# Attention and ternary FFN on one core: another order of work in the fronts of both batches

## The reference

```
q, gate = split(x @ Wq)          # 8 heads of 64, and a gate of the same width
k, v    = x @ Wk, x @ Wv         # 2 key/value heads of 64, each for 4 query heads
q, k    = rotary(q), rotary(k)   # on 16 of the 64 features of a head
o       = softmax(q k^T / 8) v   # full attention over 2048 keys
x       = layernorm(x + (o * silu(gate)) @ Wo)
h       = bitlinear(x, w_fc) + 0.05 * x @ v_lr^T @ fast_b^T @ u^T     # hidden 1024
x       = layernorm(x + bitlinear(relu(h)^2, w_proj))
```

## Time and profile before

| | us |
|---|---|
| median of 3 runs | 1777.85 (1777.14 to 1778.02) |
| the profiled execution | 1775.12 |
| its span, first to last instruction | 1773.3 |
| TensorE busy | 1670.2 (94%) |
| VectorE busy | 1390.5 (78%) |
| GpSimd busy | 989.9 (56%) |
| ScalarE busy | 742.0 (42%) |
| first score matmul of batch 0 / of batch 1 | 91.52 / 957.60 |
| mean granted TensorE clock | 0.972 of full |

### The profile page before, as it was taken

How to read it: one execution, slowest core, us unless ns; L and a number is a source line. 1 busy time by engine, 2 the same in 40 slices (tenths; PEclk the granted TensorE clock), 3 DMA queues, 4 the chain that set the end, 5 groups by cost and what they waited for, 6 DMA issues and landing times.

```text
span 1773.3 us, 26408 instructions
## 1 busy us (share of the span) xinstructions
PE 1670.2 (94%) x6902; PEld 817.4 (46%) x6902; DVE 1390.5 (78%) x1692; ACT 742.0 (42%) x1407; POOL 989.9 (56%) x765
## 2 busy tenths in 40 slices
PE   5699999999999999999868999999999999999996
PEld 3444444444444444447744444444444444444585
DVE  6668888888888888757766788888888888885587
ACT  1244444444444444444422444444444444445352
POOL 0546666666666665653334566666666666657342
PEclk8799999999999999999987999999999999999998
DMA  4600101000000000020043010000000000000001
GB/s 163 159 18 23 23 23 24 22 22 22 23 22 22 22 20 19 1 78 24 25 115 84 18 29 23 23 23 22 22 22 23 22 22 22 19 1 1 25 25 48
DMA packets 36916, 59.76 MB, mean 34 GB/s; under 512 B 6624, under 2 KB 17264, under 8 KB 36288
## 3 DMA queue, kind: packets, MB, share of 16 engines
q1 hardware_dynamic: 36800, 58.50, 12.6%
HBM read 20.07 MB, written 4.19 MB: 14 GB/s over the span
## 4 chain that ended last, share of the span: by engine, by line
PE 75%; DVE 10%; issue 8%; ACT 2%; DMA 2%; POOL 1%; SPq 1%; DVEq 0%; ACTq 0%; POOLq 0%
PE ob L578 24%; PE trio L566 16%; PE trio L567 11%; PE sc L533 8%; PE trio L513 6%; PE trio L672 3%; DVE acc L328 2%; PE trio L589 2%; DVE maxp L1059 2%; PE sc L639 2%; ACT probs L824 2%; DMA acc<-in_x 1%; PE ob L687 1%; PE trio L687 1%; PE trio L525 1%
## 5 line engine op out<-in xcount | busy, mean ns | idle before, releaser
L328 POOL TENSOR_TENSOR acc<-acc,probs 128x512 f32<-128x512 f32 x448 | 577.2, 1288 | 435.1 <-DVE acc L328 377.2
L824 ACT ACTIVATE probs<-trio 128x512 f32<-128x512 f32 x1024 | 530.0, 603 | 654.5 <-PE trio L567 556.4
L1059 DVE TENSOR_REDUCE maxp<-sc 128x2 f32<-128x1024 f32 x472 | 575.1, 1218 | 138.6 <-PE sc L535 137.1
L578 PE MATMUL ob<-probs,v_sb 128*64 128x512 f32 x2048 | 495.8, 605 | 0.0
L328 DVE TENSOR_TENSOR acc<-acc,probs 128x512 f32<-128x512 f32 x448 | 429.9, 960 | 81.3 <-ACT probs L824 76.7
L566 PE MATMUL trio<-qa,kab 128*128 128x512 f32 x1024 | 459.8, 449 | 3.6 <-DMA qb<-mrow 3.6
L567 PE MATMUL trio<-qb,kab 128*128 128x512 f32 x1024 | 405.0, 396 | 0.0
L566 PEld LDWEIGHTS trio<-qa,kab 128*128 128x128 f32 x1024 | 192.4, 188 | 322.6 <-issue 210.7
L578 PEld LDWEIGHTS ob<-probs,v_sb 128*64 128x64 f32 x2048 | 123.9, 136 | 241.6 <-issue 178.8
L533 PE MATMUL sc<-kab,qa 64*128 64x512 f32 x512 | 197.1, 460 | 29.1 <-DVE maxp L1198 16.0
L567 PEld LDWEIGHTS trio<-qb,kab 128*128 128x128 f32 x1024 | 194.1, 190 | 23.4
(11 more groups left out here) (122 smaller groups left out, 1420.4 us busy)
## 6 DMA issues: line engine op xcount, KB each, us to landing
qa<-high_sb SPq DMA_DIRECT2D x128, 128.0 KB, 2.3
qb<-low_sb SPq DMA_DIRECT2D x64, 128.0 KB, 2.3
tables_sb<-in_tables SPq DMA_DIRECT2D x34, 128.0 KB, 2.4
xT_sb<-in_xT SPq DMA_DIRECT2D x2, 2048.0 KB, 10.2
acc<-in_x SPq DMA_DIRECT2D x8, 512.0 KB, 4.2
out_y<-acc SPq DMA_DIRECT2D x8, 512.0 KB, 3.1
kab<-acc SPq DMA_DIRECT2D x24, 128.0 KB, 2.4
rot_sb<-raw_sb SPq DMA_DIRECT2D x72, 32.0 KB, 1.8
```

What stands on the lines that cost most here:

```text
L328: ops.tensor_tensor(total, total, part, ALU.add).then_inc(summed, 1)
L578: mm = nc.tensor.matmul(ob[hd * D:(hd + 1) * D, :], v_sb[:, t, kv * D:(kv + 1) * D], probs[:, t % RING, hd * CHUNK:(hd + 1) * CHUNK], star ...
L824: nc.scalar.activation(probs[:, t % RING, hd * CHUNK:(hd + 1) * CHUNK], score_bank(t, hd), ACT.Exp, scale=float(D) ** -0.5).then_inc(probs ...
L1059: nc.vector.tensor_reduce(two_columns(p, j), MAX_PAIRS[j % 2], AX_X, ALU.max).then_inc(maxed, 1)
```

## The change

The two fronts get another order, and some of their work another engine; the arithmetic stays.

- **Loads by first use.** SP loads k weights, the first 512 columns of x, w_fc, the q weights of pair 0, then x in chunks; w_proj, v weights, the rest of wq and wo follow between the first swaps. Five small loads go onto ScalarE's queue. Semaphores are split so that each user waits for its own load.
- **Set-up inside the front.** The low-rank product, the transposes and their copies stand between the stages and the maxima of front 0; in between go the first projections.
- **Front order** k0, q0, k1, k2, k3, q1, q2, and all rotary work on GpSimd, with the low part of a stage behind the rotary work of later ones.
- **High parts first.** A stage's two high parts that the maxima need (`k_early`, `q_early`) are placed by ScalarE right behind the rounding; they have their own semaphore, and the maxima wait for it alone. The other four placements stay on SP (`place_rest`), and the scores of a unit wait for them.
- **Stage q2** is rounded, split and placed in the first unit of attention.
- **Unrolled**: both batches, and all 128 cycles of attention of each.
- **Next batch in the FFN.** The first two projections of batch 1 stand on TensorE between the up and the down matmuls of the last chunk of batch 0; their copies follow on ScalarE behind the last squares, their swaps on SP ahead of the store of that chunk's output.

```diff
-    for i in range(HEAD):
-        emit(0, i // CYCLES, i % CYCLES)
-    with eng.Fori(0, NCH - 1) as c:
-        for i in range(HEAD, HEAD + PAIRS * CYCLES):
-            emit(c, i // CYCLES, i % CYCLES)
-    for i in range(HEAD, PAIRS * CYCLES):
-        emit(NCH - 1, i // CYCLES, i % CYCLES)
+    for unit in range(UNITS):
+        for y in range(CYCLES):
+            emit(unit // PAIRS, unit % PAIRS, y)
...
+        FRONT = [("k", 0, 0), ("q", 0, 1), ("k", 1, 2), ("k", 2, 3), ("k", 3, 0), ("q", 1, 1), ("q", 2, 0)]
...
+        def place_early(eng, stage, b, targets):
+            slot = stage[0]
+            eng.wait_ge(rounded[slot], done(uses(stage, b) + 1))
+            for part, hd, dst in targets:
+                eng.dma_start(raw_words(dst), raw_words(part[slot][hd * D:(hd + 1) * D])).then_inc(early[slot], 16)
...  (SP)
+            sp.dma_start(wk_sb[:, :, :], ...).then_inc(k_loaded, 16)
+            load_x(0, 0)
             sp.dma_start(wfc_nat, w_fc.rearrange("(j p) c -> p j c", p=P)).then_inc(wfc_loaded, 16)
+            sp.dma_start(wqg_sb[:, :, 0:P], wq_v[:, :, 0:P]).then_inc(q_loaded, 16)
+            load_x(0, 1)
+            sp.wait_ge(tables_cleared, 2)
...
+                front_tables(4, b)
+                front_swap(4, b)
+                front_rest(0, b)
+                front_tables(5, b)
+                front_rest(1, b)
+                front_swap(5, b)
+                front_rest(2, b)
+                front_rest(3, b)
+                front_rest(4, b)
+                front_tables(6, b)
+                front_swap(6, b)
+                sp.wait_ge(ones_set, 3)
                 place_max(b, 0, 0)
+                front_rest(5, b)
...  (TensorE)
+            for b in range(BATCH):
+                if b == 0:
+                    front_project(0, b)
+                    front_project(1, b)
+                    setup_gated_rank()
+                front_project(2, b)
+                front_project(3, b)
+                if b == 0:
+                    setup_low_rank()
+                    setup_wfc_transposes()
+                front_project(4, b)
+                front_project(5, b)
...
                 front_maxima(0)
+                if b == 0:
+                    setup_wp_transposes(0)
+                else:
+                    v_half(2, b)
                 front_maxima(2)
...
+                max_transpose(b, 0, 0, ob[:, :])
                 for i in range(2, LEAD):
                     front_pair(1, i)
+                if b == 0:
+                    v_half(5, b)
+                    v_half(6, b)
+                    v_half(7, b)
+                    front_project(6, b)
...
+                    if c == NCH - 1 and b < BATCH - 1:
+                        front_project(0, b + 1)
+                        front_project(1, b + 1)
                     ffn_down(first_n + c, range(JT - 2))
...  (ScalarE, batch 0)
+                    front_round(0, b)
+                    setup_wfc_copies()
+                    front_round(1, b)
+                    front_round(2, b)
+                    front_copy(4, b)
+                    setup_wp_copies(0)
+                    front_round(3, b)
+                    setup_wp_copies(1)
+                    setup_scale_copy()
+                    front_copy(5, b)
+                    front_round(4, b)
+                    copy_v(0, b)
+                    copy_v(1, b)
+                    front_round(5, b)
+                    copy_v(2, b)
+                    front_copy(6, b)
+                    copy_v(3, b)
...  (GpSimd)
+                front_rope(0, b)
+                front_rope(1, b)
+                front_rope(2, b)
+                front_low(0, b)
+                front_rope(3, b)
+                front_low(1, b)
+                front_rope(4, b)
+                front_low(2, b)
+                front_low(3, b)
+                front_rope(5, b)
+                front_low(4, b)
+                front_low(5, b)
+                front_rope(6, b)
```

More of the change, by code:

```diff
@@ L510, in project, with setup_scale_row @@
+            def setup_scale_row():
+                pe.wait_ge(q_copied, done(5))
+                for i in range(2):
+                    mm = nc.tensor.matmul(trio[i * D:(i + 1) * D, 0, 0:HID], ones[:, :], wp_scale[:, :],
+                                          start=True, stop=True)
+                mm.then_inc(setup_pe, 1)
             def project(w, col, chunk, semaphore, bank):
@@ L741, in _ @@
+                for slot in range(SLOTS):
+                    stage = front([0, 1, 2, 3][slot]) if slot else front(4)
+                    pe.wait_ge(placed[slot], placed_before(stage, b, 1))
+                pe.wait_ge(ones_set, 3)
+                pe.wait_ge(q_copied, done(b * STAGES + PRO))
                 pe.wait_ge(v_copied, done((b + 1) * TILES))
@@ L748, in _ @@
                 first_n = b * NCH
+                pe.wait_ge(wo_loaded, 16)
                 output_projection(first_n, 0)
@@ L781, in _ @@
[L781 to L786 removed]
+            act.dma_start(fbT_sb, fast_bT).then_inc(small_loaded, 16)
+            for dst, src in ((v_lr_sb, v_lr), (gate_sb[:, :], gate), (uT_sb, uT), (ident[:, :], ident_in)):
+                act.dma_start(dst, src).then_inc(small_loaded, 16)
@@ new lines, in setup_gate, with setup_wfc_copies @@
+            def setup_gate():
+                act.wait_ge(small_loaded, 16 * 5)
+                act.wait_ge(setup_pe, 1)
+                nc.scalar.activation(bv_sb, sc[0:RANK, 3, 0:HID], ACT.Copy, scale=gate_sb[0:RANK, 0:1])\
+                  .then_inc(setup_act, 1)
+            def setup_wfc_copies():
+                act.wait_ge(setup_pe, 3)
+                for h in range(HC):
+                    for q in range(2):
+                        last = nc.scalar.copy(wfcT[:, h, q * CHUNK:(q + 1) * CHUNK], sc[:, 2 * h + q, :])
+                last.then_inc(setup_act, 1)
@@ new lines, in setup_wp_copies, with setup_scale_copy, copy_stage @@
+            def setup_wp_copies(half):
+                act.wait_ge(setup_pe, 4 + half)
+                for q in range(2):
+                    j = 4 * half + 2 * q
+                    last = nc.scalar.copy(wpT[:, j:j + 2, :], V_BANKS[q].rearrange("p (a c) -> p a c", a=2))
+                last.then_inc(setup_act, 1)
+            def setup_scale_copy():
+                act.wait_ge(setup_pe, 6)
+                nc.scalar.copy(wp_scale[:, :], trio[:, 0, 0:HID]).then_inc(setup_act, 1)
+            def copy_stage(stage, number, b, bank):
@@ L833, in emit @@
                     exponential(b, c, p, 2 * y + 1)
+                    if y == 0 and first(c, p):
+                        round_stage(front(6), b)
                     if y == 0 and behind_exists(c, p):
@@ new lines, in front_round @@
+            def front_round(s, b):
+                what, n = FRONT[s][0:2]
+                if b >= 1 and s == 1:
+                    act.wait_ge(ffn2_ready, done(2 * b * NCH))
+                if b >= 1 and s == 2:
+                    act.wait_ge(res_done, done(b * NCH * TILES))
+                if s == 3:
+                    act.wait_ge(y_stored, 16 * (NCH * b + 1))
+                round_stage(front(s), b)
+                place_early(act, front(s), b, k_early(n) if what == "k" else q_early(n))
@@ L946, in emit @@
                     add_exponentials(pool, nc.gpsimd, b, c, p, 2 * y + 1, 0, sum_a, sum_b)
+                    if y == 1 and first(c, p):
+                        rope_low(nc.gpsimd, front(6), b)
                     if y == 1 and behind_exists(c, p):
```

438 lines of the change are left out of this document (246 added, 192 removed).

## The result

The kernel after takes **1691.38 us** (median of 4 runs, 1690.12 to 1692.52), the kernel before 1777.49 us (1777.04 to 1778.02) beside it; the ratio is 0.9515 with a 95% interval of 0.9499 to 0.9532. The forecast was 1736 us (1717 to 1757): the change gained 86 us, twice the 42 forecast.

The account below looks back on a forecast made before the run. Attention was taken as bound by TensorE's own stream, the fronts by chains across engines. Front 0 -20, front 1 -22 and attention 0 gave -42 from 1775.12: 1733, plus 2.7 for the median: 1736 us (1717 to 1757).

Parts of the forecast that it names:

- Unrolled attention: Attention's 256 cycles: neither the jump back nor fresh code costs a visible amount; 0, bounds 2 us either way.
- Front 0: Start of batch 0 up to attention: needed loads first, attention at 71.5 instead of 91.52 us, gain 20 (6 to 28).
- The tail: End of front 0: half groups, last projection, copy, swap and DMA of the maxima in sequence, 10.5 us (8.6 to 12.6).
- Front 1 with the FFN: From batch 0's FFN to batch 1's attention: ends at 935.5 instead of 957.60 us, gain 22 (13 to 27).
- The batch loop: Jump between batches: ScalarE's 2.86 us wait for issue on front 1's chain goes, contained in front 1's sum.
- the early projections: k0 and q0 of batch 1 inside the last FFN chunk: first rotary operation at 896.5 us against 908.31.
- Rival 1: Front 0 keeps most of its length, 83 us instead of 71.5, at the lower clock: 1749 us; chance 0.13.
- Rival 2: More than forecast: both fronts at best bounds (55 us), or forecast plus 11 us of inner jumps: 1723 us; chance 0.10.
- Rival 3: Early parts land no earlier because the DMA engines are the limit; gain 19, 1759 us; chance 0.05.
- Rival 4: Slower: fetching straight code costs 2.86 us for each of 36 added blocks, 1839 us; chance 0.04.

Follow-up runs that it names:

- b_order: Kernel before, loops kept, with ScalarE's wait for the scores written behind its three ring waits instead of ahead of them: 1750.06 us, ratio 0.9858.
- b_all: Kernel before with its batch loop and its loop over chunks written out on all five engines, nothing else changed: 1724.19 us, ratio 0.9714.
- a_noffn: Kernel after with projections k0 and q0 of batch 1 moved from inside the FFN's last chunk to behind the FFN: 1690.76 us, ratio 0.9526.
- b_conly: Kernel before with only the loop over chunks written out, the batch loop kept: 1773.13 us, ratio 0.9981.
- a_gate6: Kernel after with the maxima of both fronts waiting again for all six placements of a stage: 1718.47 us, ratio 0.9677.
- b_bonly: Kernel before with only the batch loop written out, the loop over chunks kept: 1766.60 us, ratio 0.9950.
- a_cloop: Kernel after with the loop over chunks put back around attention on all engines, batches still written out: 1746.93 us, ratio 0.9835.

## Why the prediction was wrong

**The step that failed is *Unrolled attention*, taken as 0 with bounds of 2 us; it was 45.7 us.** It looked for the loop's price at the jump and compared the first pass of the body with the second. But both passes run the same register instructions, so the comparison could not show their price; it showed, rightly, that the jump was free. What the unrolling took away was two instructions in each of 256 cycles, on ScalarE between the scores and the exponential (0.15 us, 38.6 us in the waits of b_order), and others on VectorE. The prediction had named units other than 43.2 to 43.6 us as a sign that it is wrong; they are 41.8.

**The reading that excluded it** was "TensorE is busy 43.14 of 43.65 us, so attention is its own stream, with 0.5 us idle a unit". After, the same work is busy 41.68 us: 1.5 us of the busy time was waiting that the profile counts as busy. (The matmuls of L566, whose weight loads wait for the exponential, took 0.449 us on the mean before and 0.429 after: 20 us in all.) The Trainium skill ("Perfetto Trace Analysis", Identifying the Most-Contended Engine) says that busy time of matmuls is a poor measure of how near TensorE is to its limit, since pipelined ones look shorter in a trace; the two rows agree that it is poor, by 1.46 us a unit, though here the busy time was too long. The view that did show it lay in the trace of before: 88.3 us of waits of weight loads for ScalarE. The Trainium skill ("Advanced Engine Details and Errata", Sequencer Loop) has the engine's instructions wait in a queue for their semaphores, while a control instruction is run by the sequencer; b_order agrees, where the exponential that itself carries the wait starts 0.15 us sooner.

**Front 0** was right: -20 forecast, -19.4 measured; projections from 6.06 us (6 forecast), maxima from 35.79 (35.5), attention at 72.16 (71.5). The tail was as the order said: the last projection, its swap, and only then the DMA of the maxima (70.09).

**Front 1 with the FFN** was right in size, not in its pacing: -22 forecast, -19.3 measured (-24.6 and +5.3). Two of its terms were wrong. The batch loop, priced at ScalarE's 2.86 us, is worth 4.7 in b_all. And the end was worked out along GpSimd's stages, almost without idle time, with q1 last. q1 was last, but GpSimd stood 4.8 us in three waits for swaps (1.67 of them at 883.58), the last two of them behind the store on SP, and VectorE's sixteen maxima ended beside it (891.95). So the early projections, from which the sum starts, buy nothing (a_noffn), and that the size came out is in part luck.

**The rivals.** Rival 1 falls with front 0. Rival 2 (1723) named the inner jumps, which cost next to nothing in the kernel before (b_conly is 3 us faster): it came nearer, by a cause that isn't there. Rival 3 (fronts that end at 80 and 950) falls with both fronts and with a_gate6: the early parts do land earlier. Rival 4 falls: the kernel after fetched 55 and 53 packets of instructions on two queues, the kernel before 38 and 78, and no wait for them shows in attention.

**Open.** Why TensorE's instructions were still loaded at some jumps back and were fetched again at others (none in the kernel before, one of two in each batch of b_bonly, all in a_cloop). The price is shown, 4.6 to 8.3 us a unit. The Trainium skill ("Runtime: NRT & Kernel Launch", Instruction fetch mechanics) says that a jump to a page that isn't loaded stalls for its fetch; the packets on queue 8 agree, at the slow jumps and by their absence at the free ones.

## What to carry to other kernels

In a loop, look for instructions between a wait that is on the path and the instruction that it is for, and write the wait that is met last as the last one, so that the instruction itself carries it; or write out the loops, all of them: with the inner one left, some or all of its jumps cost 5 to 8 us each (b_bonly, a_cloop). Don't take TensorE's busy share for proof that it paces a stage: ask the waits of its weight loads what they wait for. A comparison of two passes through a loop can't show a cost that both contain.

## What was not expected of the hardware

- An instruction between a met wait and the instruction that it is for: about 0.075 us each on ScalarE (0.156 us for two, 0.230 for three), 0.083 on VectorE ahead of the eight rows. The view of waits shows it, the busy time doesn't.
- A jump back where TensorE's instructions were fetched again: 5.1 us without an instruction on TensorE at the first of a_cloop (3.1 at that of batch 0 in b_bonly), then 8 us at a granted clock of 0.67 on the mean. Where nothing was fetched, the jump cost nothing to see.
- Two passes of 64 rows back to back take 0.66 us; one with other matmuls on both sides takes 0.43.
- VectorE's eight operations of L1241 took 8.35 us beside GpSimd's rotary stages in front 0; the same eight took 3.26 before, with GpSimd idle. The next eight (L1254), which read PSUM, took 3.22 in both kernels. No run takes the two engines apart, so the cause is not shown.
